# Edge units in pairs, row loads in two pieces and spread first loads in a graph and transformer kernel

## What is computed

```python
m = x[src] * rel[edge_type]                      # 53125 edges' ends, twice (rel1, rel2)
m = concat([m[:half] @ W_in, m[half:] @ W_out])
agg = segment_sum(m / deg[dst], dst)
h = h + res * tanh(agg + x @ W_loop + b)         # two convolutions, then h @ mu_w + mu_b
for i in range(4):                               # the mix
    h = layernorm(x); x = x + linear_attention(h, Wq, Wk, Wv, Wo, bo)
    h = layernorm(x); x = x + gelu(h @ W1 + b1) @ W2 + b2
xn = layernorm(x); x = x + graph(xn) + mix(xn)
x = x + ffn(layernorm(x))                        # shared(x) + gated top 2 of 4 experts
```

## Time and profile before

| what | us |
|---|---|
| runs (3), median | 1947.61 |
| lowest, highest | 1944.21, 1951.19 |
| profiled execution | 1951.01 |
| its span, first to last instruction | 1949.2 |
| TensorE busy (matmuls) | 1757.6 |
| VectorE busy | 1223.5 |
| ScalarE busy | 628.7 |
| GpSimd busy | 1300.5 |

### The profile page before, as it was taken

One profiled execution on the slowest core, in us unless ns is written; L12 is line 12 of the kernel. 1 busy time (PEld: TensorE's weight loads), 2 busy tenths in 40 slices (PEclk: granted clock), 3 DMA queues, 4 the chain that ended last, 5 costly groups with the idle time before them and its releaser, 6 DMA issues. The chain is left out here.

```text
span 1949.2 us, 28362 instructions
## 1 busy us (share of the span) xinstructions
PE 1757.6 (90%) x9423; PEld 1294.2 (66%) x9423; DVE 1223.5 (63%) x3583; ACT 628.7 (32%) x1552; POOL 1300.5 (67%) x1297
## 2 busy tenths in 40 slices
PE   2788999998899999989999978987998998988998
PEld 1355867776587777758777645655776676766787
DVE  6777455664756576575556464487665666478766
ACT  4442233343233434333333332231221222222333
POOL 6776777777777777777777733755777676666300
PEclk9999999999899999999999999999999999999999
DMA  9667666667766666776666764667867565555301
GB/s 250 196 200 234 195 207 192 200 191 224 245 197 207 204 193 202 220 248 196 192 203 209 210 192 127 188 197 215 241 192 214 183 202 184 167 176 179 108 14 27
DMA packets 195923, 371.44 MB, mean 191 GB/s; under 512 B 39343, under 2 KB 127445, under 8 KB 195780
## 3 DMA queue, kind: packets, MB, share of 16 engines
q0 software_dynamic: 74304, 220.71, 39.0%
q1 hardware_dynamic: 93124, 126.68, 20.2%
q10 hardware_dynamic: 28352, 22.24, 4.2%
HBM read 305.39 MB, written 64.95 MB: 190 GB/s over the span
## 5 line engine op out<-in xcount | busy, mean ns | idle before, releaser
L1049 POOL DMA_INDIRECT xg<-h_rows,idx_tab x416 | 426.8, 1026 | 205.9 <-issue 125.1
L1049 POOL DMA_INDIRECT xg<-xn_rows,idx_tab x416 | 432.7, 1040 | 141.6 <-issue 123.4
L1001 POOL DMA_INDIRECT rg<-relation_rows,idx_tab x416 | 417.2, 1003 | 136.4 <-issue 126.2
L2880 PE MATMUL ps_hid<-hT,wff 128*128 128x250 f32 (+1 forms) x1920 | 372.3, 347 | 7.0 <-ACT gT L2314 7.0
L2892 PE MATMUL ps_down<-wff,gT 128*125 128x256 f32 x1600 | 366.1, 382 | 0.0
L2880 PEld LDWEIGHTS ps_hid<-hT,wff 128*128 128x128 f32 x1920 | 313.7, 192 | 59.1 <-issue 27.0
L1144 DVE TENSOR_TENSOR xg<-xg,rg 128x256 f32<-128x256 f32 x832 | 296.6, 418 | 71.4 <-DMA xg<-h_rows,idx_tab 40.1
L2892 PEld LDWEIGHTS ps_down<-wff,gT 128*125 128x125 f32 x1600 | 295.4, 189 | 46.3 <-issue 5.1
L2751 PE MATMUL ps_seg<-xg,hot 128*61 128x257 f32 (+1 forms) x1664 | 233.9, 404 | 39.3 <-DVE xg L1144 34.3
L2314 ACT ACTIVATE gT<-ps_hid,b1p 128x250 f32<-128x250 f32 (+1 forms) x480 | 176.8, 434 | 286.6 <-PE ps_hid L2880 286.4
L2751 PEld LDWEIGHTS ps_seg<-xg,hot 128*61 128x61 f32 (+1 forms) x1664 | 103.1, 139 | 134.6 <-issue 67.3
(11 more groups left out here) (382 smaller groups left out, 2420.5 us busy)
## 6 DMA issues: line engine op xcount, KB each, us to landing
second_relation_rows<-rg SPq DMA_DIRECT2D x104, 512.0 KB, 4.0
rg<-second_relation_rows SPq DMA_DIRECT2D x104, 512.0 KB, 4.0
wff<-L_mix_W ACTq DMA_DIRECT2D x8, 1024.0 KB, 7.2
rg<-relation_rows,idx_tab POOLq DMA_INDIRECT x416
xg<-xn_rows,idx_tab POOLq DMA_INDIRECT x416
xg<-h_rows,idx_tab POOLq DMA_INDIRECT x416
h_rows<-qT_all SPq DMA_DIRECT2D x25, 64.0 KB
qrow<-h_rows ACTq DMA_DIRECT2D x25, 64.0 KB
```

What stands on the lines that cost most here:

```text
L1001: pool.indirect_dma_start(rg[:, k, :], None, rel_d, indices(step, 1)).then_inc(s_edge[k // UNIT], 16)
L1049: pool.indirect_dma_start(xg[:, k, 0:D], None, rows, indices(step, 0)).then_inc(s_edge[k // UNIT], 16)
L2880: ins = pe.matmul(hidden, w1[:, c, ff * P:(ff + 1) * P], hT[:, a:z, c, :], start=c == 0, stop=c == KC - 1)
```

## The change

Three edits. (1) Marks are rounded up to even numbers of units (at most n), and the middle of two marks on TensorE is rounded down to even, so that units stand two by two. (2) Loads of a tile's rows into `h_rows` and into `qrow` take two DMAs of 64 partitions each, into buffers widened to 128 partitions, the second of which brings three rows more than the tile has; the last tile keeps three. Stores keep three. Waits count accordingly (`loaded`). (3) ScalarE's joint of layer 3 no longer holds the loads of h1 and x: x's stand behind the first gelu of layer 2's group 4, the wait for the stored h1 behind the second gelu of layer 3's group 0, and the loads of its five tiles two, two and one behind gelus 2, 3 and 4. A variable on SyncE is renamed.

```diff
--- before.py
+++ after.py
@@ -265,9 +265,9 @@
             assert free_at[0] <= 3 * GT * KC * T
             return v
         staged = [free_piece(D)[0:T, :] for _ in range(SLOTS)]
-        h_rows = [free_piece(D)[0:T, :]]
+        h_full = [free_piece(D)]
         in_q = free_piece(2 * KC * D)
-        h_rows += [free_piece(D)[0:T, :] for _ in range(AHEAD - 3)]
+        h_full += [free_piece(D) for _ in range(AHEAD - 3)]
         free_rest = free_q[:, free_at[0]:]
         h_new = [free_piece(D)[0:T, :] for _ in range(SLOTS)]
         assert AW + D + T + KC * T <= free_rest.shape[1]
@@ -276,7 +276,8 @@
         def pieces(v, n):
             return [v[:, m * KC * D:(m + 1) * KC * D].rearrange("p (c n) -> p c n", c=KC) for m in range(n)]
         wg = [[*pieces(in_q, 2), wloop[:, :, :]], pieces(in_qkv, 3)]
-        qrow = sb("qrow", [T, GT, D])
+        qrow_full = sb("qrow", [P, GT, D])
+        qrow = qrow_full[0:T, :, :]
 
 
         kx5s = [kx5p[0:T], wff[0:T, 0:GT * (D + AW)].rearrange("p (j n) -> p j n", j=GT)]
@@ -294,7 +295,8 @@
         seed = sb("seed", [T, GT], I32)
         rstd = sb("rstd", [T, GT])
         tmp = sb("tmp", [T, GT])
-        h_rows += [ctxT[0:T, :, :].rearrange("p c n -> p (c n)"), hTa[0:T, :, :, :].rearrange("p s c t -> p (s c t)")[:, 0:D]]
+        h_full += [ctxT[:, :, :].rearrange("p c n -> p (c n)"), hTa[:, :, :, :].rearrange("p s c t -> p (s c t)")[:, 0:D]]
+        h_rows = [b[0:T, :] for b in h_full]
         mu_b = zeros[:, 0:D]
         qrows = [qrow, xh]
 
@@ -701,7 +703,7 @@
             if dense_before(lay, gi):
 
                 at = dict(up0=1, up1=2, down0=3, up2=5, down1=7, up3=9, down2=10, up4=13, down3=14, ctx=15, end=16)
-            return {m: -(-n * k // at["end"]) for m, k in at.items()}
+            return {m: min(-(-n * k // (2 * at["end"])) * 2, n) for m, k in at.items()}
 
 
         def bank_parts(j, hf):
@@ -730,7 +732,7 @@
 
         def dense_loads(h):
 
-            return len(range(h, NT, AHEAD)) if h < AHEAD else 0
+            return loaded(range(h, NT, AHEAD)) if h < AHEAD else 0
 
         def dense_before(lay, gi):
             return (lay, gi) == (DENSE_LAYER, DENSE_GROUP)
@@ -786,6 +788,16 @@
             for a, z in PIECES:
                 ends = rows[a:z], tile_rows(dram, t, a, z)
                 eng.dma_start(*(ends[::-1] if store else ends)).then_inc(done, 16)
+
+        def load_tile(eng, full, dram, t, done):
+            if t == NT - 1:
+                move_tile(eng, full[0:T, :], dram, t, done)
+            else:
+                eng.dma_start(full[0:64, :], dram[ds(WIDTH[0] * t, 64), :]).then_inc(done, 16)
+                eng.dma_start(full[64:P, :], dram[ds(BASE[1] + WIDTH[1] * t, 64), :]).then_inc(done, 16)
+
+        def loaded(tiles):
+            return sum(MOVED if t == NT - 1 else 32 for t in tiles)
 
         def move_group(eng, rows, dram, gi, done, store=False):
             for a, z in PIECES:
@@ -865,7 +877,7 @@
             def load_h(t):
                 if t >= AHEAD:
                     sp.wait_ge(s_hn, t + (1 - AHEAD))
-                move_tile(sp, h_rows[t % AHEAD], xn_d, t, s_hx[t % AHEAD])
+                load_tile(sp, h_full[t % AHEAD], xn_d, t, s_hx[t % AHEAD])
 
             def store_h1(t):
                 sp.wait_ge(s_hn, t + 1)
@@ -919,8 +931,8 @@
                 sp.wait_ge(s_msg, UNITS + (u + 1) + 1)
                 sp.dma_start(rg2[:, u % RU * BLOCK:(u % RU + 1) * BLOCK, :].rearrange("p s d -> p (s d)"),
                              rel2_d[u:u + 1].rearrange("o p n -> p (o n)")).then_inc(s_r2ld[u % RU], 16)
-            loaded = (at_group[L - 1, 1] - STEPS2) // UNIT
-            for u in range(loaded):
+            ahead = (at_group[L - 1, 1] - STEPS2) // UNIT
+            for u in range(ahead):
                 load_relations(u)
             sp.wait_ge(s_cw, L)
             sp.dma_start(sW1, rows_of(io["L0_ffn_sW1"])).then_inc(s_ew, 16)
@@ -936,7 +948,7 @@
             ):
                 sp.dma_start(t, src, allow_slow_non_contiguous=True).then_inc(s_ew, 16)
             more = (at_last - STEPS2) // UNIT
-            for u in range(loaded, more):
+            for u in range(ahead, more):
                 load_relations(u)
             sp.wait_ge(s_b2, L * NG)
             sp.dma_start(b2_b[:, :], io["L0_ffn_sb3"].partition_broadcast(T), allow_slow_non_contiguous=True).then_inc(s_ew, 16)
@@ -2470,17 +2482,10 @@
                     act.dma_start(mu_w, rows_of(io["L0_gnn_mu_w"])).then_inc(s_wo, 16)
                     for t, src in ((gW, rows_of(io["L0_ffn_gW"])), (gateb, io["L0_ffn_gb"].partition_broadcast(T))):
                         act.dma_start(t, src, allow_slow_non_contiguous=True).then_inc(s_emw, 16)
-                    for k in range(SLOTS):
-                        act.wait_ge(s_h1[k], MOVED * (len(range(k, NT, SLOTS)) + 1))
-                    for t in range(GT):
-                        load_h1(t)
-                    for st in s_r2st:
-                        act.wait_ge(st, 16 * (UNITS // RU) + 16)
-                    move_group(act, x_again, io["x"], 0, s_x5)
                 act.wait_ge(s_w1, (la + 1) * 32)
 
             def load_h1(t):
-                move_tile(act, qrow[:, t % GT, :], h1_d, t, s_hx[t % GT])
+                load_tile(act, qrow_full[:, t % GT, :], h1_d, t, s_hx[t % GT])
 
             def sums_turned(k):
                 if not 0 <= k < NB:
@@ -2535,7 +2540,14 @@
                 n = Feed(lay, gi + 1) if not is_last(gi) else None
                 b.gelu(0)
                 aside(0)
+                if (lay, gi) == (L - 2, NG - 1):
+                    for st in s_r2st:
+                        act.wait_ge(st, 16 * (UNITS // RU) + 16)
+                    move_group(act, x_again, io["x"], 0, s_x5)
                 b.gelu(1)
+                if (lay, gi) == (L - 1, 0):
+                    for k in range(SLOTS):
+                        act.wait_ge(s_h1[k], MOVED * (len(range(k, NT, SLOTS)) + 1))
                 if is_first(gi):
 
                     b.norm_out(3, GT)
@@ -2554,12 +2566,18 @@
                     f.norm_out(2)
                 aside(3)
                 b.gelu(2)
+                if (lay, gi) == (L - 1, 0):
+                    load_h1(0)
+                    load_h1(1)
                 if f:
                     f.k_out(2)
                     f.q_out(2)
                     f.norm_out(3)
                 aside(4)
                 b.gelu(3)
+                if (lay, gi) == (L - 1, 0):
+                    load_h1(2)
+                    load_h1(3)
                 if f:
                     f.k_out(3)
                     f.q_out(3)
@@ -2569,6 +2587,8 @@
                 aside(5)
                 aside(6)
                 b.gelu(4)
+                if (lay, gi) == (L - 1, 0):
+                    load_h1(4)
                 aside(7)
                 if dense_behind(lay, gi):
                     dense(f)
@@ -3066,7 +3086,7 @@
 
                 def up(j, before, name=None):
                     a, z = m[before] if before else 0, m[name or f"up{j}"]
-                    b.up(j, upto, ((a + z) // 2, z))
+                    b.up(j, upto, ((a + z) // 4 * 2, z))
                 up(0, None)
                 aside(0)
                 up(1, "up0")
@@ -3223,7 +3243,7 @@
                     turned = transpose_rows(pe, ps_sums[i % 2], staged[i % SLOTS])
                     if t >= 0:
                         h = t % AHEAD
-                        pe.wait_ge(s_hx[h], (t - h) // AHEAD * MOVED + MOVED)
+                        pe.wait_ge(s_hx[h], loaded(range(h, t + 1, AHEAD)))
                         turned = transpose_rows(pe, ps_sums[i % 2][:, KC * T:2 * KC * T], h_rows[h])
                     turned.then_inc(s_dtr, 1)
 
@@ -3267,7 +3287,7 @@
                 turned = transpose_rows(pe, ps_x2[:, 0:KC * T], sums2[k % 2])
                 if t >= 0:
                     h = t % GT
-                    pe.wait_ge(s_hx[h], (dense_loads(h) + t // GT + 1) * MOVED)
+                    pe.wait_ge(s_hx[h], dense_loads(h) + loaded(range(h, t + 1, GT)))
                     turned = transpose_rows(pe, ps_x2[:, KC * T:2 * KC * T], qrow[:, h, :])
                 turned.then_inc(s_dtr, 1)
 
```

## The result

The changed kernel takes 1993.12 us (median of 6 runs, 1981.55 to 1996.20); the kernel before, run beside it, 1944.96 us (6 runs, 1938.20 to 1951.19). The direction was forecast; the forecast time, 1954 us with a range up to 1967, was not. The profiled execution took 1984.4 us, 33.4 us more than that of before, so the trace accounts for most of the difference, not for all: four of the other runs are 9 to 12 us longer than the profiled one, at mean granted clocks of 0.956 to 0.958 where it has 0.961.

What follows compares the result with a forecast made beforehand. TensorE was taken as the bound, busy 1757.6 us of a 1949.2 us span. Gains and layer 3's -17.5 us summed to -6.7 us, so 1954 us against the 1947.6 median; range 1930 to 1967, the forecast's own 1948 to 1961.

Steps and rivals of the forecast that it cites:

- the term for layer 3's pairs: Layer 3, groups 2 to 4: VectorE's dense pieces wait behind late-landing units; 17.5 us slower, bounds -28 and +5.
- The saving of a trip: TensorE, each dropped trip to a unit: 0.34 us saved; 67 fewer trips give 23 us if nothing else moves.
- Groups 2 and 3 of layer 3: Fifth and seventh units' late landings delay VectorE's L1871 and L1887, so TensorE waits: -7 us and -6 us.
- Group 4 of layer 3: Same raised marks as groups 2 and 3, but landings less late: 4.5 us slower.
- Group 1 of layer 3: Marks the same as before, only loses trips: 4 x 0.34 = 1.4 us faster.
- The lower clock: Layer 3, groups 2 to 4: lower granted clock behind long waits, counted only within the -28 us bound.
- Layers 0 to 2: Pairs there: +0.6 us together up to layer 2's late landing, +0.5 us in group 4 of layer 2.
- rival 3: Regular groups: VectorE's 0.15 us of slack isn't there, 12 us lost over 9 groups, 1966 us; chance 0.13.
- The loads in two pieces: Dense stage: SyncE issues fewer DMAs, 2.63 us a tile; 7 us faster, bounds +1 and +11.
- rival 2: Dense stage waits for stores, not issues, so two-piece loads pay nothing there: 1961 us; chance 0.12.
- The spread loads: Layer 3's first group: ScalarE's 7.04 us wait moves to VectorE; +0.8 us with 4 trips fewer, bounds -2 and +10.
- Rival 1: Layer 3's fifth and seventh units are not late: faster, 1932 us, or 1909 with all cover intact; chance 0.25, 0.05 at 1909.

## Why the prediction was right and wrong

**The step that failed** is the term for layer 3's pairs: -17.5 us for groups 2 to 4, of which -4.5 for group 4, and +1.4 for group 1, with the lower clock behind the new waits put at nothing. Pairs in layer 3 alone cost 46 us. In the trace of the changed kernel groups 1 to 4 lost 38 us: 29.6 of waits and 15.3 of clock not granted, less 7.1 in the rest. All other stretches together were 4.5 us faster, where 9.4 was forecast. The direction and the place were right, and not by luck: the forecast named the fifth unit's landing ahead of VectorE's dense pieces. The sizes were not.

**The saving of a trip** was forecast at 0.34 us and is 0.28 where it can be read without a change of clock: 19 us for all 67 rather than 23. The blocks behind a unit, which I had taken as equal to those in front, are the likely difference; that wasn't measured by itself.

**Groups 2 and 3 of layer 3** came out at -7.1 and -6.4 us against -7 and -6, partly by luck. In group 3 TensorE's wait for the bias, forecast at 5 us, was 4.2 (the line for kx L1883 above), and the waits behind the later pairs grew by 3.8 us. But its wait at L1887, forecast at 5 us, fell from 3.3 to 2.4. In group 2 there is no wait at all at the first of either; waits for units' products went from 2.1 to 4.0 us, one of 2.6 us for rows (L1891) is new, and half of its growth is a clock that the term didn't have. Nor is the size steady: the same group 3 lost 12.5 us in the trace with layer 3's pairs alone.

**Group 4 of layer 3**: 4.5 us forecast, 17.4 measured, and 17.4 again in the trace where it alone had pairs. I had taken it as a milder case of group 3 because VectorE had no wait for the fifth unit's rows there. That was so because VectorE took the unit up late, at 1630.28, and not because its rows came early: GpSimd asks for them 3.2 us into the group in both kernels. Even so the start, with bias and normalisation, has only 3.8 us more of waits, near the forecast. What the term left out are the later places of the group, 9.0 us of waits, and the clock, 8.5 us.

**Group 1 of layer 3**: +1.4 us forecast as a gain, 7.0 lost. "The same marks" hid that the halves move: the step took trips as the only thing that changes. A unit 1.7 us later on TensorE is a gather 1.7 us later, into a burst of 640 KB. That burst is shown for nearly half of the loss; the rest is open.

**The lower clock** stood only in a bound. Clock not granted grew by 18.8 us, 17.1 of them in layer 3. I had the row for it and counted it once, for the wait that goes, and not for the ones that come. At the rate of that row, 1.8 us behind 7.04 us of wait, groups 2 to 4 would have come to some -22 us (an estimate); at the measured rate, half a us of clock for each us of wait, to -26; they lost 30.9.

**Layers 0 to 2**: +0.6 and +0.5 forecast; pairs there alone are 5 us slower, not clear of zero. In the regular groups of layer 1 the saving came (0.7 of the 1.0 us) and the slack of 0.1 to 0.2 us was right (0.12 us more of waits each), which is where rival 3 fell. Missed was the unit that `down2 + 1` adds before kmax.

**The loads in two pieces**: +7 forecast, some 4 measured, or 3 by the traces; a piece of 64 rows takes longer to issue than a third of three, and a tile takes 3.3 us and not 2.6. The premise that SyncE's issues set the pace holds for fewer tiles than I took. With an interval of 0.9952 to 1.0003, rival 2 (nothing) isn't ruled out. **The spread loads**: +0.8 in group 0 forecast, -0.1 measured, by the wait that was named: VectorE's xh.

Rival 1 named the point that decides, the landing of the fifth unit, and fell on it. The large misses are all to one side: what the edits remove I had priced from a row, and what they delay by comparison with a neighbour.

## What to carry to other kernels

A unit that is bundled with its neighbour is also asked for earlier by one engine and given back later by another: count, for every mark that moves, what is behind it in each queue, all through the group and not only at its start, also inside callbacks like `one(m["down2"] + 1)`. Where a ring of four ties a gather to its consumer, the fifth unit's rows come a gather's whole time after the first unit is done (9 us in group 4 here, 1634.47 to 1643.52), however the units are bundled; what must not happen is that another engine's work stands behind that fifth unit. Price each new wait of a few microseconds with the granted clock behind it, and pair work only in the stretches whose trace has slack: here six groups out of twenty.

## What the runs showed of the hardware

- With 640 KB of DMAs issued among them, the rows of a gathered unit landed 7.1 us after its last gather; with them behind it 3.5 us. Between 1401 and 1408 the DMA engines' busy share was 1.00. Moving the DMAs took VectorE's wait from 6.74 to 3.13 us.
- New waits came with a lower granted clock: 18.8 us of clock not granted beside 37.8 us of waits in the changed kernel, 23.9 beside 33.8 in layer 3 with its pairs alone. Some 15 of the 18.8 us lengthened TensorE's instructions (an estimate from its busy time). The stretch ahead of layer 0, which the edits hardly touch, had 0.4 to 5.0 us more of it in the traces of after and of the experiments than in that of before, so a growth of that size in a single trace isn't the edit's.
- Two issues of 64 rows take 0.49 and 0.64 us of SyncE's queue, each counted to the next issue; the three pieces of a store took 1.66 us in that kernel and 1.53 before.
